# A transformer block on one core: four down-weight sums made ahead of the third attention tile, and the mean subtracted on ScalarE in the tail

## What is computed

```python
x = x + layernorm(attention(layernorm(x), Wqkv, bqkv, Wo, bo))
x = x + layernorm(ffn(layernorm(x), W_gate, W_up, W_down))

def attention(x):                       # one head, width 256
    q, k, v = split(x @ Wqkv + bqkv)
    return softmax(q @ k.T / 16) @ v @ Wo + bo
def ffn(x):
    return (silu(x @ W_gate.T) * (x @ W_up.T)) @ W_down.T
def layernorm(x):
    return (x - mean(x)) / sqrt(var(x) + 1e-5)
```

## Time and profile before

| | us |
|---|---|
| Median of 3 runs | 1697.21 (1696.9 to 1697.76) |
| Profiled execution, device time | 1697.39 |
| Its span, first to last instruction | 1695.6 |
| TensorE busy | 1655.5 (98%) |
| VectorE busy | 1114.7 (66%) |
| ScalarE busy | 631.4 (37%) |
| GpSimd busy | 515.5 (30%) |

### The profile page before, as it was taken

How to read it: one execution, slowest core, us unless ns; L and a number is a source line. 1 busy time by engine, 2 the same in 40 slices (tenths; PEclk the granted TensorE clock), 3 DMA queues, 4 the chain that set the end, 5 groups by cost and what they waited for, 6 DMA issues and landing times.

```text
span 1695.6 us, 20962 instructions
## 1 busy us (share of the span) xinstructions
PE 1655.5 (98%) x7672; PEld 1374.0 (81%) x7672; DVE 1114.7 (66%) x1605; ACT 631.4 (37%) x1141; POOL 515.5 (30%) x430
## 2 busy tenths in 40 slices
PE   6899999889999999999999999999999999999997
PEld 5788888778888888888888888888888888888886
DVE  7965687667876666666657776955565555654666
ACT  3232444334633333333346544432333333244550
POOL 3520355765164444454211101611121111200005
PEclk9999999999999999999999999999999999999999
DMA  7220466876744545454579665744444454487772
GB/s 288 112 87 7 170 230 201 262 241 231 255 176 157 180 171 168 143 168 153 184 253 332 238 204 187 263 156 141 140 135 148 150 164 152 140 294 239 232 231 99
DMA packets 161665, 317.09 MB, mean 187 GB/s; under 512 B 12960, under 2 KB 41760, under 8 KB 158624
## 3 DMA queue, kind: packets, MB, share of 16 engines
q1 hardware_dynamic: 161568, 315.82, 55.5%
HBM read 212.21 MB, written 103.56 MB: 186 GB/s over the span
## 4 chain that ended last, share of the span: by engine, by line
PE 88%; DVE 5%; POOL 4%; DMA 1%; ACT 1%; issue 1%; SPq 0%; POOLq 0%; DVEq 0%; ACTq 0%
PE ps L341 27%; PE ps L342 27%; PE ps L343 27%; PE ps L1939 2%; PE ps L1832 2%; PE ps L1884 2%; PE ps L1940 1%; PE ps L1885 1%; DVE probs_t L1299 1%; DVE bank_max L1448 1%; DMA xc_raw<-xq_dram 1%; DVE y_all L1747 1%; DVE norm_x_stats L1280 0%; POOL y_all L943 0%; DMA norm_rows<-stats_dram 0%
## 5 line engine op out<-in xcount | busy, mean ns | idle before, releaser
L1299 DVE TENSOR_TENSOR slots<-w_raw,slots 128x512 fp32r<-128x512 f32 x500 | 408.9, 840 | 264.0 <-ACT slots L1111 263.8
L1111 ACT CAST slots<-w_raw 128x512 fp32r<-128x512 f32 x504 | 301.7, 621 | 464.8 <-PE ps L343 459.1
L341 PE MATMUL ps<-xc,slots 128*128 128x512 f32 x1208 | 470.9, 390 | 0.6 <-DVE u L1623 0.6
L343 PE MATMUL ps<-xc,slots 128*128 128x512 f32 x1208 | 470.1, 389 | 0.0
L342 PE MATMUL ps<-xc,slots 128*128 128x512 f32 x1208 | 470.0, 389 | 0.0
L341 PEld LDWEIGHTS ps<-xc,slots 128*128 128x128 f32 x1208 | 226.8, 188 | 47.8 <-DVE u L1623 1.0
L343 PEld LDWEIGHTS ps<-xc,slots 128*128 128x128 f32 x1208 | 226.7, 188 | 47.3
L342 PEld LDWEIGHTS ps<-xc,slots 128*128 128x128 f32 x1208 | 226.8, 188 | 46.8
L341 PE MATMUL ps<-slots 128*128 128x512 f32 x572 | 222.6, 389 | 0.0
L343 PE MATMUL ps<-slots 128*128 128x512 f32 x572 | 222.5, 389 | 0.0
L342 PE MATMUL ps<-slots 128*128 128x512 f32 x572 | 222.5, 389 | 0.0
(11 more groups left out here) (187 smaller groups left out, 2419.8 us busy)
## 6 DMA issues: line engine op xcount, KB each, us to landing
w_raw<-hsp_dram SPq DMA_DIRECT2D x154, 256.0 KB, 3.8
hsp_dram<-hs SPq DMA_DIRECT2D x20, 1792.0 KB, 8.4
w_raw<-wffn SPq DMA_DIRECT2D x134, 256.0 KB, 3.6
w_raw<-wffn SPq DMA_DIRECT2D x66, 512.0 KB, 6.2
w_raw<-wdt_dram SPq DMA_DIRECT2D x88, 256.0 KB, 3.7
wgt_dram<-tt SPq DMA_DIRECT2D x21, 1024.0 KB, 8.3
w_raw<-wgt_dram SPq DMA_DIRECT2D x84, 256.0 KB, 2.7
wdt_dram<-tt SPq DMA_DIRECT2D x11, 1024.0 KB, 5.3
```

Of the source, the lines that this page charges most:

```text
L341: pe.matmul(dst, stat(HIGH), mov(HIGH), start=first, stop=False, skip_group_check=reread)
L343: return pe.matmul(dst, stat(LOW), mov(HIGH), start=False, stop=last, skip_group_check=reread)
L1111: act.copy(operand(n, HIGH), source(n)).then_inc(w_high, 1)
L1299: return dve.tensor_tensor(dst, src, high.bitcast(F32), ALU.subtract)
```

## The change

GpSimd makes `down_sums(0)` to `down_sums(3)` (`EARLY` = 4) before `attend(2)`, then `down_sums(4)` at the end of `attend(2)`, behind `sum_x1(0)`, and `down_sums(t + 2)` in tiles 3 to 8. SP stores groups 0 to 3 and loads weights 2 to 5 before its loop over tiles.

In the tail, VectorE also makes the negated mean of each bank. ScalarE adds it to both halves as a bias, while GpSimd makes the root, and VectorE multiplies by the root and adds the residual in one operation per half. GpSimd makes no residual sum there any more, and SP stores each half by itself. VectorE waits for `y_summed` = 12 ahead of the first bank. The semaphore `late_normed` is replaced by `x1n_done`, which counts on from the attention stage.

```diff
--- before.py
+++ after.py
@@ -163,6 +163,7 @@
     return KP - 1 if p == MIXED else (p - 1) // 2
 
 
+EARLY = 4
 LATE_LOAD, LATE_STATS, LATE_NORM, LATE_MORE, LATE_STORE = 2, 3, 4, 5, 6
 
 
@@ -245,6 +246,7 @@
     row_max = tiny("row_max", [1])
     neg_max = tiny("neg_max", [1])
     bank_sum = tiny("bank_sum", [4])
+    neg_mean = tiny("neg_mean", [TPB])
     row_sum = tiny("row_sum", [1])
     inv_sum = tiny("inv_sum", [1])
 
@@ -316,7 +318,7 @@
     xc_loaded = [sem(f"xc_loaded{i}") for i in range(7)]
     s1_done, s2_done, s3_done, s4_done = sem("s1_done"), sem("s2_done"), sem("s3_done"), sem("s4_done")
     xc_high, a11_low, xc_low = sem("xc_high"), sem("a11_low"), sem("xc_low")
-    late_loaded, late_normed = sem("late_loaded"), sem("late_normed")
+    late_loaded, mean_negated = sem("late_loaded"), sem("mean_negated")
 
     rest_loaded = sem("rest_loaded")
     w_loaded = [sem("w_loaded0"), sem("w_loaded1")]
@@ -538,6 +540,9 @@
             load_wd(0)
             load_wd(1)
             load_residual(1)
+            for k in range(EARLY):
+                store_wdt(k)
+                load_wd(k + 2)
             for t in range(2, TILES):
                 if t == TILES - 1:
                     sp.wait_ge(q_low, TILES)
@@ -545,10 +550,11 @@
                     sp.wait_ge(s_ready, 4 * TILES)
                     load_xc(0, A12, 0, 1)
                     load_xc(0, A22, 1, 1)
-                if t - 2 < KP:
-                    store_wdt(t - 2)
-                    if t < KP:
-                        load_wd(t)
+                k = t - 2 + EARLY
+                if k < KP:
+                    store_wdt(k)
+                    if k + 2 < KP:
+                        load_wd(k + 2)
                 if t == KP + 1:
                     load_rest()
                     load_pair(1, pair_buffer(0))
@@ -738,12 +744,12 @@
                 load_operand(n)
             for i in range(TPB):
                 store_out(1, 0, i)
-            for i in range(TPB - 1):
-                store_out(1, 1, i)
-            for h in range(HALF):
-                sp.wait_ge(y_summed, 15 + h + 1)
-                sp.dma_start(out[S - P:S, cols(h, BANK)], y_all[:, YC21 + h, TPB - 1, :]).then_inc(out_stored, 16)
-            sp.wait_ge(out_stored, 16 * (TILES + 1))
+            for i in range(TPB):
+                for h in range(HALF):
+                    sp.wait_ge(y_summed, 8 + TPB + 2 * i + h + 1)
+                    sp.dma_start(out[row_block(BLOCKS - 1, i), cols(h, BANK)],
+                                 y_all[:, YC21 + h, i, :]).then_inc(out_stored, 16)
+            sp.wait_ge(out_stored, 16 * (TILES + TPB))
         @block.gpsimd
         def _(pool):
             pool.memset(ident[:], 0.0).then_inc(ident_cleared, 1)
@@ -870,8 +876,9 @@
                 if 3 <= t < TILES - 1:
                     rstd(norm_l, t - 3, 0)
                     pool.wait_ge(x1n_done, t - 2)
-                if t - 2 < KP:
-                    down_sums(t - 2)
+                k = t - 2 + EARLY
+                if t > 2 and k < KP:
+                    down_sums(k)
                 if t == KP + 2:
                     pair_sums(1, pair_buffer(0))
                 if t == KP + 3:
@@ -881,7 +888,11 @@
                     first_sums(t - 2 * TPB - 1)
                 rstd(norm_a, t - 2, 0)
                 sum_x1(t - 2)
-
+                if t == 2:
+                    down_sums(k)
+
+            for k in range(EARLY):
+                down_sums(k)
             for t in range(2, TILES):
                 attend(t)
 
@@ -977,7 +988,6 @@
             out_block(1, 0)
             rstd_y(1, 1, 0)
             for i in range(1, TPB):
-                sum_y(1, 1, i - 1)
                 rstd_y(1, 1, i)
         @block.scalar
         def _(act):
@@ -1272,6 +1282,12 @@
                 act.copy(y_all[:, YC21, i, :], ps[:, 4 + i, :]).then_inc(c21_copied, 1)
             gates(1)
             downs(1)
+            for i in range(TPB):
+                act.wait_ge(mean_negated, i + 1)
+                for h in range(HALF):
+                    src = y_all[:, YC22, i, :] if h else ps[:, 4 + i, :]
+                    act.activation(y_all[:, YC21 + h, i, :], src, ACT.Identity,
+                                   bias=neg_mean[:, i:i + 1]).then_inc(yn_done, 1)
         @block.vector
         def _(dve):
             def row_stats(norm, i, src):
@@ -1674,7 +1690,7 @@
                     moments(norm_l, 0)
                 i = late_tile(p, LATE_NORM)
                 if i is not None and j == 0:
-                    normed(norm_l, LNT + i, 0, res[:, 1, :], late_normed)
+                    normed(norm_l, LNT + i, 0, res[:, 1, :], x1n_done)
 
             def last_attention_tiles(j):
                 if j == 0:
@@ -1797,32 +1813,27 @@
                     src = ps[:, 4 + i, :]
                 dve.bn_stats(norm_y.stats[:, i, h, :], src).then_inc(norm_y.stats_done, 1)
 
-            def last_norm(i, h, done=None):
-                src = y_all[:, YC22, i, :] if h else ps[:, 4 + i, :]
-                op = dve.tensor_scalar(y_all[:, YC21 + h, i, :], src, norm_y.moments[:, 0, i:i + 1],
-                                       norm_y.rstd[:, i:i + 1], ALU.subtract, ALU.mult)
-                if done is not None:
-                    op.then_inc(done, 1)
+            def last_sum(i, h):
+                dve.wait_ge(yn_done, 8 + TPB + 2 * i + h + 1)
+                y = y_all[:, YC21 + h, i, :]
+                dve.scalar_tensor_tensor(out=y, in0=y, scalar=norm_y.rstd[:, i:i + 1],
+                                         in1=last_res[:, i, cols(h, BANK)], op0=ALU.mult,
+                                         op1=ALU.add).then_inc(y_summed, 1)
 
             for i in range(TPB):
                 last_stats(i, 1)
+            dve.wait_ge(last_res_loaded, 16)
+            dve.wait_ge(y_summed, 8 + TPB)
             for i in range(TPB):
                 last_stats(i, 0)
                 dve.wait_ge(norm_y.stats_done, 2 * (8 + TPB) + TPB + i + 1)
                 moments(norm_y, i)
+                dve.wait_ge(norm_y.moments_done, 8 + TPB + i + 1)
+                dve.tensor_scalar(neg_mean[:, i:i + 1], norm_y.moments[:, 0, i:i + 1], -1.0, None,
+                                  ALU.mult).then_inc(mean_negated, 1)
                 dve.wait_ge(norm_y.rstd_done, 8 + TPB + i + 1)
-                if i < TPB - 1:
-                    last_norm(i, 0)
-                    last_norm(i, 1, yn_done)
-                else:
-                    dve.wait_ge(last_res_loaded, 16)
-                    dve.wait_ge(y_summed, 8 + TPB + TPB - 1)
-                    for h in range(HALF):
-                        last_norm(i, h, yn_done)
-                    for h in range(HALF):
-                        dve.wait_ge(yn_done, 8 + TPB + i + 1 + h)
-                        y = y_all[:, YC21 + h, i, :]
-                        dve.tensor_tensor(y, y, last_res[:, i, cols(h, BANK)], ALU.add).then_inc(y_summed, 1)
+                for h in range(HALF):
+                    last_sum(i, h)
         @block.tensor
         def _(pe):
             pe.wait_ge(ident_ready, 1)
@@ -2070,7 +2081,7 @@
             def transpose_late(i, g):
                 p = 4 * i + LATE_NORM + g
                 if g == 0:
-                    pe.wait_ge(late_normed, i + 1)
+                    pe.wait_ge(x1n_done, LNT + i + 1)
                 pe.wait_ge(u2_done, p + 1)
                 transposes(4 * (p % 2) + 1, KH * g, res[:, 1, :], KH).then_inc(xq_ready, 1)
```

## The result

The changed kernel takes 1703.27 us (median of 6 runs, 1701.88 to 1703.94), the kernel before beside it 1697.24 (1695.66 to 1697.76): a measured ratio of 1.0031 with a 95% interval of 1.0021 to 1.0041 (the two medians alone give 1.0036). It is slower, and the whole interval lies above 1.002. The forecast was 1700.7 with a range of 1697.9 to 1706.0, so the time lies in the range and 2.6 us above the forecast. The profiled execution took 1702.9 us with a span of 1700.7, 5.5 and 5.1 us more than before.

What follows compares the result with a forecast made beforehand. The prediction took GpSimd as the bound of tiles 9 to 12 and TensorE of the others. Its terms, +21.0 + 0.4 - 13.3 - 4.6 = +3.5 us, gave 1700.7 us, range 1697.9 to 1706.0.

Steps and rivals of the forecast that it cites:

- The early groups: Ahead of tile 2: extra sum groups on GpSimd cost 10.3 us each, making TensorE 21.0 us late (16.5 to 22.5).
- The five landings: Early groups' stores: each next group waits for one to land, 5.1 us after issue; five count.
- The slack of 0.49: Attention tiles: VectorE can spare 0.49 us of a late `a_norm`, and hands on the rest to TensorE one for one.
- The clock: TensorE after the early groups' stalls: a fall to the lower clock adds 0.4 us, bounds 0 to 2.
- the first stall: Tile 2: `a_norm` waits 17.2 us for its root, and TensorE idles near 16 us.
- the second stall: Tile 3: `a_norm` starts 21.5 us late in all, which swallows the 1.7 us lost to the clock before.
- Tiles 9 to 12: Attention, four slow tiles: with the down-weight sums gone, all 13.3 us return (11.5 to 13.5).
- The tail: Last product's norm and residual: a bank takes 3.1 us, the fourth waits for TensorE; gain 4.6 us (3.5 to 4.8).
- A: Tile 3: groups 4 and 5 finish before its root is wanted, so no stall there; 1697.7 us, chance 0.10.
- B: Ahead of tile 2: the early groups fit, as stores do not hold GpSimd; 1680.7 us, chance 0.07.
- C: Attention: the restart stays at the lower clock or tiles 9 to 12 await the partner; 1703 to 1706 us, chance 0.14.
- D: Slow tiles 9 to 12 keep half their stall, something hidden holding the input sums; 1707.3 us, chance 0.03.

Runs made afterwards that it cites:

- e7_none_early: The changed kernel with no down-weight group early (`EARLY` = 0) and each group behind the residual sum at the tile's end, from tile 2: 1690.16 us, ratio 0.995.
- e1: The kernel before with only the changed kernel's new tail: 1694.07 us, ratio 0.998 to the kernel before.
- e6: The changed kernel with VectorE instead of ScalarE subtracting the mean in the tail: 1703.99 us, ratio 1.0034 to the kernel before.

## Why the prediction came out as it did

**The early groups: right.** Forecast +21.0, with 0.4 for the clock; measured +22.07. From the start of group 0 to `a_norm` of tile 3 the sum gave 233.1 - 175.50 = 57.6 us, the trace 234.69 - 176.89 = 57.8. Both waits were there, 17.28 (17.2 forecast) and 4.27, and TensorE's idle 15.77 (near 16); it resumed 2.65 us after each `a_norm` as read from the earlier trace rows. The five landings were 5.1 us each, as taken. The slack of 0.49 was kept: less the start's 1.25, `a_norm` of tile 3 is 21.85 late, and 21.85 - 0.49 = 21.36. The remaining 0.7 is the next term.

**The clock: the mechanism right, the size low.** The clock fell to 1.2 GHz with both stalls, not with the first alone. Stretches of the changed kernel, columns as in the earlier trace rows:

```profile
204.00:216.00 12.00, 0.00 (x0) 0.00 (x0) 2.11 (x6) 0.00 (x0) 6.84 (x7) 0.50 0.67 228
216.50:220.70 4.20, 4.19 (x15) 3.51 (x15) 4.13 (x8) 0.59 (x1) 3.09 (x3) 0.50 0.81 286
220.70:237.30 16.60, 13.87 (x74) 11.34 (x72) 8.12 (x19) 5.60 (x14) 10.74 (x12) 1.00 0.73 242
234.57:237.34 2.77, 0.01 (x1) 0.01 (x1) 2.62 (x7) 0.00 (x0) 1.77 (x2) 1.00 0.93 315
237.34:237.70 0.36, 0.36 (x3) 0.36 (x4) 0.36 (x1) 0.00 (x0) 0.36 (x1) 1.00 0.94 199
237.74:241.15 3.41, 3.41 (x13) 2.72 (x12) 3.41 (x8) 0.59 (x1) 0.35 (x2) 0.50 1.00 255
```

In the first stall the clock is at 0.50 while TensorE is idle and for the first 4.2 us of matmuls; the 2 us or so lost there are swallowed by the second stall, as the prediction said. In the second it is still 1.00 through the 2.77 us without work and for the first 0.4 us of matmuls, and only then at 0.50, for 3.4 us. That loss is not swallowed. From the resumption to the next scores take 250.51 - 237.34 = 13.17 us; in the kernel before, after a stall that left the clock at 1.00, 331.29 - 318.77 = 12.52. The difference of 0.65 is the term for which 0.4 was taken: the row gave 0.66 for a fall, and the prediction shaded it for the chance that none came. The rule of the Trainium skill, "TensorE: Matmul & The Clock Gate", part 1, that an idle array goes back to 1.2 GHz, is what the first stall shows. The second fits it less well: the clock fell when TensorE was already at work again. Three of the four stalls of 2 us in the kernel before left the clock at 1.00.

**Tiles 9 to 12: right.** Forecast -13.3, measured -13.3, with no wait on VectorE there. The reason given was too narrow, though: "one group of sums per tile is what tile 8 has" is true, but e7_none_early has both groups in a tile and no stall. What the profile said in the earlier trace rows was that the root queued behind the sums, and a queue can be mended by its order as well as by its length.

**The tail: the size near, one reading wrong.** Forecast -4.6, measured -4.43 in the trace, of which 0.4 is lost again outside the span, and -3.6 (-1.9 to -4.9 by the interval) in e1's medians. A bank takes 3.29 us (1684.99 to 1688.29), not 3.1: the fused operations, 0.75 each and 1.42 for the pair, are within their bounds (0.6 to 0.85), but the pair takes 1.34 to the next bank's statistics where 1.25 was taken, and it starts 1.22 us after the moments' start instead of 1.15. There ScalarE's first result (1686.16 + 0.69 = 1686.85) and the root (1686.84) come together. The prediction had the fourth bank wait for TensorE. In the trace there is no such wait; VectorE's own pace brings it to 1694.86, 0.13 after TensorE's end, and that both meet there is luck. The new wait of 0.2 us ahead of the first bank is the 0.19 of the trace. The prediction priced ScalarE's two subtractions as part of the gain without asking what they save: e6 says 0.3 us.

**The rest.** By the medians the loss is 6.0, so the forecast is 2.6 low, and one trace can't close that. Of the 2.0 us between the forecast's +3.5 and the profiled execution's +5.5, 1.25 are the start of that execution, 0.65 to 0.7 the stalls and the clock, 0.2 the tail, 0.4 the time outside the span (2.2 against 1.8), at which the prediction put nothing, less 0.4 in the feed-forward stages and 0.06 in the last store. The 0.4 in the feed-forward stages isn't explained.

**The rivals.** A (no second stall) fell with the wait of 4.27. B (the groups fit) fell with brackets of 5.2 us; it decided below a landing of 4.4, and the five that count were 5.1. C named the right size, 1703, by the wrong causes: neither a slow restart beyond the second stall's 0.65 us nor a late partner (in the trace GpSimd's input sums waited 1.44 us for `x1n`, and for no DMA). D fell with the equal stretches.

**What the prediction missed** is not in its sum. It took the place of the sums ahead of the root as given and weighed only how many to move early. The idle time of 12.06 us in the earlier trace rows takes one group more than the kernel before has there, and with the order turned round not even that one is needed.

## What to carry to other kernels

When an engine works in order and another waits for one small result of it, look first at what stands ahead of that result in the same tile, and put long work that nobody waits for behind it; that gained 13.3 us here with the engine's load unchanged, while moving four groups to an earlier place cost 22.1 us to gain the same 13.3. A block of work that refills a single buffer costs its own time plus the landing of its store each time it is repeated without something between, so multiply by the sum of both before filling an idle gap with it. In a lockstep of two engines, look for the long operation first: with it gone and the norm and sum fused, which engine subtracted the mean was worth 0.3 us of 4.4 here.

## What the runs showed of the hardware

- A store of 1 MB landed 5.1 us after its issue and held GpSimd's next sums for 5.22 to 5.23 us, three times in a row, whether TensorE worked beside it or stood still.
- TensorE was idle for 2.77 us at a clock of 1.00 and resumed at 1.00; 0.4 us later the clock fell to 0.50 for 3.4 us, while it was busy. That cost 0.65 us.
- A multiply-add of 128x512 float32 in one operation with a per-row factor (SCALAR_TENSOR_TENSOR) took VectorE 0.75 us (1.42 for a pair, whose records overlap), ScalarE's Identity with a bias 0.69 from PSUM and 0.71 from SBUF, and VectorE's lone subtraction 0.75 from PSUM and 0.48 from SBUF.
